# A graph network kernel: attention edge terms moved from the first count stage to TensorE in the gated pass, and gated sums taken in two column halves

## The reference

```python
# layer 0, gated: h = x, e = edge_attr_64
msg_in = concatenate([h[src], h[dst], e], axis=-1)
messages = (silu(msg_in @ w1 + b1) @ w2 + b2) * sigmoid(msg_in @ wg + bg)
agg = segment_sum(messages, dst) / maximum(deg, 1)
h_new = silu(concatenate([h, agg]) @ wu + bu)
# layer 1, mean: sums the features of the sources of each target
# layer 2, attention, twice (l = 1, 2): ea = edge_attr_128 plus loop rows
a_e = ea @ We_l @ ae_l                    # the attention edge term: one number per edge
alpha = leaky_relu(a_s[src] + a_d[dst] + a_e)
```

## Time and profile before

| What | Value |
|---|---|
| median of 3 runs | 2327.94 us (2326.16 to 2332.72) |
| span of the profiled execution, first to last instruction | 2030.3 us |
| median less span | 297.6 us |
| PE busy | 1709.1 us, 84% of the span |
| DVE busy | 1468.0 us, 72% |
| POOL busy | 985.4 us, 49% |
| ACT busy | 869.6 us, 43% |
| mean granted TensorE clock | 0.915 of full speed |
| gated pass, first gather to last addition of a window | 49.2 to 618.2 us of the span |
| first count stage, first DVE work to last addition | 659.4 to 962.8 us of the span |

### The profile page before, as it was taken

The page is one execution under the profiler, slowest core; times in us unless marked ns, Lnnn a source line. Parts: engine busy times, 40 slices in busy tenths (PEclk is TensorE's granted clock), DMA queues, the critical chain, the costliest instruction groups (busy, mean ns, idle before and its releaser), DMA issues. The chain is left out here.

```text
span 2030.3 us, 42546 instructions
## 1 busy us (share of the span) xinstructions
PE 1709.1 (84%) x13175; PEld 1366.7 (67%) x13175; DVE 1468.0 (72%) x4926; ACT 869.6 (43%) x2150; POOL 985.4 (49%) x998
## 2 busy tenths in 40 slices
PE   5699998989883799999557999956599999299996
PEld 5588877878773666677555887746478878166664
DVE  5788888888885899896667666655776664744656
ACT  2466655655554566564304444421154443411100
POOL 3777777777773000000366777735677775300000
PEclk9899999999996699999658999986699999699998
DMA  6877677777760245553352111108221111344542
GB/s 189 236 210 231 200 223 215 206 228 204 206 199 6 98 165 197 171 198 151 119 135 62 46 42 42 48 18 203 61 67 43 41 43 36 123 163 182 197 164 87
DMA packets 145068, 276.84 MB, mean 136 GB/s; under 512 B 28296, under 2 KB 88334, under 8 KB 141557
## 3 DMA queue, kind: packets, MB, share of 16 engines
q1 hardware_dynamic: 105102, 191.71, 29.2%
q0 software_dynamic: 35456, 79.88, 14.9%
q10 hardware_dynamic: 4278, 2.42, 0.5%
HBM read 228.82 MB, written 45.08 MB: 135 GB/s over the span
## 5 line engine op out<-in xcount | busy, mean ns | idle before, releaser
L1023 POOL DMA_INDIRECT gated_rows<-p_tab,src_idx x416 | 432.2, 1039 | 141.6 <-issue 130.6
L1387 POOL DMA_INDIRECT ring<-table,src_idx x384 | 383.9, 1000 | 146.0 <-issue 93.3
L2219 PE MATMUL bank<-counts,mean_xs 128*128 128x416 bf16 (+2 forms) x1350 | 219.6, 322 | 32.0 <-DVE mean_xs L1707 32.0
L1052 PE MATMUL bank<-gated_wide_q,gated_comb 128*128 128x256 f32 x832 | 219.7, 388 | 2.7 <-DMA gated_wide_q<-q_tab 2.7
L1121 ACT ACTIVATE gated_sig<-gated_pre 128x512 f32<-128x512 f32 x208 | 131.2, 631 | 211.4 <-DVE gated_pre L1193 208.7
L2219 PEld LDWEIGHTS bank<-counts,mean_xs 128*128 128x128 bf16 x1350 | 126.0, 97 | 116.4 <-issue 34.4
L1518 ACT COPY attention_counts<-bank 128x475 f32 (+1 forms) x224 | 127.2, 568 | 176.9 <-PE bank L1542 153.2
L1553 PEld LDWEIGHTS bank<-attention_counts,h_sb 128*128 128x128 f32 x900 | 157.7, 191 | 61.9 <-ACT attention_counts L1518 3.6
L1193 DVE TENSOR_TENSOR gated_pre<-bank,gated_rows 128x512 f32<-128x512 f32 x208 | 142.8, 687 | 74.9 <-PE bank L1052 43.7
L1553 PE MATMUL bank<-attention_counts,h_sb 128*128 128x232 f32 (+1 forms) x900 | 192.0, 341 | 2.0 <-DVE attention_counts L1610 1.5
L1542 PE MATMUL bank<-attention_wide_b,scratch 128*128 128x400 f32 x448 | 189.2, 504 | 0.0
(11 more groups left out here) (416 smaller groups left out, 3896.0 us busy)
## 6 DMA issues: line engine op xcount, KB each, us to landing
counts<-count_tabs SPq DMA_DIRECT2D x16, 2675.0 KB, 9.4
scratch<-in_edge_attr_dram SPq DMA_DIRECT2D x51, 512.0 KB, 4.1
count_tabs<-mean_counts SPq DMA_DIRECT2D x8, 2675.0 KB, 11.2
gated_relr<-rel_rows SPq DMA_DIRECT2D x104, 128.0 KB
gated_ids<-id_rows SPq DMA_DIRECT2D x26, 512.0 KB
gated_wide_q<-q_tab SPq DMA_DIRECT2D x208, 64.0 KB
attend_hot_lo<-low_hots SPq DMA_DIRECT2D x52, 256.0 KB, 3.4
gated_ea<-in_edge_attr_dram SPq DMA_DIRECT2D x51, 256.0 KB
```

The lines of the kernel that those rows point to most:

```text
L1023: pool.indirect_dma_start(out=rows[:, q % TICKS, c, :], out_offset=None, in_=p_tab, in_offset=bass.IndirectOffsetOnAxis(ap=src_idx[:, b, j ...
L1052: mm = pe.matmul(PRE[q % 2][:, c * 2 * P:(c + 1) * 2 * P], comb[:, u, k, c, :], wide_q[:, u, c, :], start=True, stop=True)
L1387: pool.indirect_dma_start(out=rows[:, n % RING, j, :], out_offset=None, in_=table, in_offset=bass.IndirectOffsetOnAxis(ap=src_idx[:, gathe ...
L2219: mm = pe.matmul(BANKS_D[q % ND][:, 0:width], xs[l][:, m // 3, m % 3, :], counts[:, s % 2, m // 3, at:at + width], start=(m == 0), stop=(m ...
```

## The change

1. In the gated pass SP also loads edge_attr_128 (512 KB per two batches, into free space of `h_sb`). `turn_ea` transposes two 128x128 blocks of it per tick beside the one of edge_attr_64, ACT copies them out with one 128x256 copy (`eaT`), and `turn_silu` ends with two f32 matmuls that have them as stationary and `ae_v` as moving operand (two columns). ACT copies the four numbers per partition to `ae`.
2. `ae_v` is made at the start of the gated pass instead of in the update; `ae_w` is gone.
3. `sum_up` swaps its operands: 64 columns of `hot` are stationary and the message with a column of ones (129 columns) is moving. The block j even writes partitions 0 to 63 of the bank, j odd partitions 64 to 127. The bf16 counting matmuls and the cast of `hot` are gone.
4. Since the result is now nodes by features in two halves, a batch needs one step more: ACT copies the bank out (`keep_sums`, 128x129), and PE multiplies that with a 128x64 matrix that adds the halves and transposes (`fold_halves`: a 64-column f32 matmul for the features, and one with a single stationary column for the counts). DVE adds the window one tick later.
5. The first count stage loses everything that made edge terms: the loads, `turn_ea`, `make_ae`, `copy_eaT`, `take_ae`, `sum_own`. SP's wait for the stored tables moves from the attention stage to the update before it.

```diff
@@ gated_pass
+            ea128 = flat(h_sb[:, :, :])[:, J * P:J * P + UN * J * P].rearrange("p (b j d) -> p b j d", b=UN, j=J)
+            eaT = sb("eaT", [P, TRN, 2, P])
...
-                        pe.transpose(EAT[:, 0:P], ea64[:, u, 2 * k:2 * k + 2, :].rearrange("p j d -> p (j d)"),
-                                     ident[:, :]).then_inc(ea_turned, 1)
+                        pe.transpose(EAT[:, 0:P], ea64[:, u, 2 * k:2 * k + 2, :].rearrange("p j d -> p (j d)"), ident[:, :])
+                        for c in range(2):
+                            mm = pe.transpose(EAT[:, (1 + c) * P:(2 + c) * P], ea128[:, u, 2 * k + c, :], ident[:, :])
+                        mm.then_inc(ea_turned, 1)
...
-                            mm = pe.transpose(ST[:, c * P:(c + 1) * P], silu[:, q % 2, c, :], ident[:, :])
+                            pe.transpose(ST[:, c * P:(c + 1) * P], silu[:, q % 2, c, :], ident[:, :])
+                        for c in range(2):
+                            mm = pe.matmul(ST[:, 2 * (P + c):2 * (P + c) + 2], eaT[:, q % TRN, c, :], ae_v[:, :], start=True, stop=True)
...
-                        for c in range(2):
-                            j = 2 * k + c
-                            pe.matmul(SEG[b % 2][:, 0:W], msg[:, q % 2, c, :], hot[:, u, j, :],
-                                      start=(j == 0), stop=(j == J - 1), skip_group_check=True)
-                        for c in range(2):
-                            j = 2 * k + c
-                            mm = pe.matmul(SEG[b % 2][:, W:2 * W], ones_b[:, :], hot_b[:, u, j, :],
-                                           start=False, stop=(j == J - 1), skip_group_check=True)
+                        for c, half in ((0, low), (1, high)):
+                            mm = pe.matmul(SEG[b % 2][half, 0:P + 1], hot[:, u, 2 * k + c, :], msg[:, q % 2, c, :],
+                                           start=(k == 0), stop=(k == PAIRS - 1), skip_group_check=True)
                         mm.then_inc(summed, 1)
+                    def fold_halves(b):
+                        pe.wait_ge(seg_ready, b + 1)
+                        pe.matmul(SEG[b % 2][:, FEATS], seg_s[:, b % 2, 0:P], fold[:, :], start=True, stop=True)
+                        pe.matmul(SEG[b % 2][0:1, DEGREES], seg_s[:, b % 2, P:P + 1], fold[:, :], start=True, stop=True).then_inc(folded, 1)
...
+                            if i > 7 and (i - 7) % PAIRS == PAIRS - 1:
+                                fold_halves((i - 7) // PAIRS)
                             if 0 <= i - 6 < NQ:
                                 sum_up(i - 6)
...
+                        reach(act, s_turned, q - TRN + 1)
+                        act.copy(flat(eaT[:, q % TRN, :, :]), EAT[:, P:3 * P]).then_inc(eaT_ready, 1)
...
+                        act.copy(ae[:, :, b, 2 * k:2 * k + 2], ST[:, 2 * P:2 * P + 4].rearrange("p (c l) -> p l c", l=2))
...
-                        act.copy(hot_b[:, b % UN, :, :], hot[:, b % UN, :, :]).then_inc(hot_b_ready, 1)
+                    def keep_sums(b):
+                        act.wait_ge(summed, (b + 1) * PAIRS)
+                        reach(act, folded, b - 1)
+                        act.copy(seg_s[:, b % 2, :], SEG[b % 2][:, 0:P + 1]).then_inc(seg_ready, 1)
@@ mean_build
-                        for at in pe_due(n):
-                            copy_eaT(at)
...
-                            for at in pe_due(n):
-                                turn_ea(at)
-                                if at > 0:
-                                    make_ae(at - 1)
                             count(n)
...
-                        if n is not None:
-                            for at in own_due(n):
-                                sum_own(at)
```

More of the change, by code:

```diff
@@ L161, in build_program @@
     place_a, origin_a = sb("place_a", [1, NSB * ATP], I32), sb("origin_a", [1, LAST], I32)
-    OWN = [i for i in range(10) if i % 2]
-    BY_PE = [i for i in range(SB_BATCHES) if i not in OWN]
-    assert BY_PE == [0, 2, 4, 6, 8, 10, 11, 12]
     ae_v, ae = sb("ae_v", [P, 2]), sb("ae", [P, 2, NB, J])
-    ae_w = sb("ae_w", [P, 2, P])
     w_tab, w_c = sb("w_tab", [P, NB, J]), sb("w_c", [P, NB, J])
@@ L690, in _ @@
                     clear_spent(sp)
-                    if gate:
-                        for k in range(2):
-                            sp.dma_start(we_g[:, k, :], a[f"L2_gnn_We{k + 1}"]).then_inc(ae_in, 16)
-                            sp.dma_start(ae_c[:, k:k + 1], a[f"L2_gnn_ae{k + 1}"].rearrange("(p a) -> p a", a=1)).then_inc(ae_in, 16)
+                    if not gate:
+                        for k in range(TABS):
+                            sp.wait_ge(table_stored[k], 16 * len(range(k, NSB, TABS)))
                 @block.gpsimd
@@ L714, in _ @@
                         mm.then_inc(a_made, 1)
-                        if gate and g == 1:
-                            pe.wait_ge(ae_in, 16 * 4)
-                            for k in range(2):
-                                mm = pe.transpose(bank[6][:, k * P:(k + 1) * P], we_g[:, k, :], ident[:, :])
-                            mm.then_inc(ae_turned, 1)
-                        if gate and g == 2:
-                            pe.wait_ge(ae_taken, 2)
-                            for k in range(2):
-                                pe.matmul(bank[6][:, k * P:(k + 1) * P], ae_b[:, k, :], we_T[:, k, :], start=True, stop=True)
-                                mm = pe.matmul(bank[6][:, (2 + k) * P:(2 + k) * P + 1], we_T[:, k, :], ae_c[:, k:k + 1], start=True, stop=True)
-                            mm.then_inc(ae_made, 1)
                 @block.scalar
@@ L905, in gated_pass @@
             loaded, ready = sem("loaded"), sem("ready")
-            ea64_in = [sem(f"ea64_in{u}") for u in range(UN // LB)]
+            ea64_in, ea128_in = [[sem(f"{n}_in{u}") for u in range(UN // LB)] for n in ("ea64", "ea128")]
             relr_in = [sem(f"relr_in{u}") for u in range(UN // LB)]
@@ L1031, in _ @@
                     pe.wait_ge(loaded, 16 * 6)
-                    pe.wait_ge(ready, 3)
+                    pe.wait_ge(ready, 5)
                     pe.wait_ge(split, 5 + 6)
                     pe.wait_ge(we_placed, 2)
+                    pe.wait_ge(ae_in, 16 * 4)
+                    for l in range(2):
+                        mm = pe.transpose(bank[7][:, l * P:(l + 1) * P], we_g[:, l, :], ident[:, :])
+                    mm.then_inc(ae_turned, 1)
+                    pe.wait_ge(ae_taken, 1)
+                    for l in range(2):
+                        mm = pe.matmul(bank[7][:, (2 + l) * P:(2 + l) * P + 1], we_T[:, l, :], ae_c[:, l:l + 1], start=True, stop=True)
+                    mm.then_inc(ae_made, 1)
+                    pe.wait_ge(ae_taken, 2)
                     def turn_ea(q):
@@ L1922, in apply @@
                                 mm.then_inc(applied, 1)
-                    def turn_ea(n):
-                        b = pe_batch(n)
-                        pe.wait_ge(ea_in[b // LB % (ER // LB)], 16 * (b // ER + 1 + (2 if b // LB * LB + LB == NB else 0)))
-                        reach(pe, eaT_ready, n)
-                        for j in range(J):
-                            mm = pe.transpose(EAT[:, j * P:(j + 1) * P], ea128[:, b % ER, j, :], ident[:, :])
-                        mm.then_inc(ea_turned, 1)
-                    def make_ae(n):
-                        pe.wait_ge(eaT_ready, n + 1)
-                        if n == AE_COUNT:
-                            pe.wait_ge(ae_taken, 1)
-                        b = pe_batch(n) % HALF
-                        for j in range(J):
-                            at = b * J + j
-                            mm = pe.matmul(AE[:, at:at + HALF * J + 1:HALF * J], eaT[:, n % 2, j * P:(j + 1) * P], ae_v[:, :], start=True, stop=True)
-                        mm.then_inc(ae_made, 1)
                     for k, w, size, n in block_steps(M_BLOCKS):
@@ L2394, in _ @@
                         load_lows(g)
-                    if l == 1:
-                        for k in range(TABS):
-                            sp.wait_ge(table_stored[k], 16 * len(range(k, NSB, TABS)))
                     for g in range(2, N3, 3):
```

175 lines of the change are left out of this document (51 added, 124 removed).

## The result

The changed kernel takes 2314.52 us (median of 6 runs, 2310.6 to 2321.94), the kernel before in the same comparison 2333.93 us (6 runs). The ratio is 0.9912, 95% interval 0.9889 to 0.9935: some 20 us faster. The forecast was 2346 us.

The account below looks back on a forecast made before the run. POOL's gathers were taken to bound the gated pass, full PE and DVE the count stage. With PE becoming the pass's bound, +102 us there and -84 us in the count stage gave +18 us, 2327.9 to about 2346 us; range 2294 to 2408 us.

Parts of the forecast that it names:

- B in full: Gated pass: the two half-sum matmuls overlap fully, 0.22 us instead of 0.45 per tick; 2299 us, chance 0.14.
- B in part: Gated pass: only one pass of each half-sum matmul overlaps, 0.34 us instead of 0.45; 2323 us, chance 0.22.
- Taken as unchanged: Whole kernel: 297.6 us around the profiled span stay as before, added to the new span of 2048 us.
- POOL's 2.69 us per tick: Gated pass before: POOL's gathers set the tick; PE's own pace is 2.23 us, leaving it some 0.46 us slack.
- PE's tick of 3.05 us: Gated pass after: PE's work sums to 3.05 us per tick, above POOL's 2.69, so PE becomes the bound.
- the halves: Gated pass: two f32 summing matmuls of 129 moving columns cost PE 0.45 us per tick, bounds 0.22 and 0.79.
- a change of the tiling mode drains TensorE: Gated pass: switching to narrow stationaries priced at zero; the rival with a drain adds 67 us, 2413 us, chance 0.14.
- Neither can hide behind the other, and ACT is near: First count stage: DVE at 0.84 and PE at 0.85 us a step; removing edge terms gives -84 us, bounds 68 and 95.
- Rival D: Count stage: DVE and ACT as near the bound as PE, giving back 68 us or less; 2362 us, chance 0.11.
- E: Gated pass: added work nearly hides behind POOL's gathers, tick 2.72 us; kernel at 2278 us, chance 0.04.
- the gathers that wait for DVE's L1193 line: Gated pass, sign of the forecast in the profile after: POOL's gathers wait for DVE and are no longer continuous.
- idle time ended by ACT: Gated pass, sign against the forecast: PE having such idle time would make the whole account wrong.

Follow-up runs that it names:

- e6: Kernel before, with the gated pass's gathers replaced by plain transfers of consecutive rows; 2144.07 us, ratio 0.9133.
- e7: Changed kernel, with the gated pass's gathers replaced by plain transfers of consecutive rows; 2236.29 us, ratio 0.9519 to the kernel before.
- e4: Changed kernel, with ACT's register reads in the count stage 8 at a time, not 26; 2296.74 us, ratio 0.9777 to the kernel before.
- e8: Kernel before, with ACT's register reads in the count stage 8 at a time, not 26; 2348.44 us, ratio 0.9982.
- e10: Kernel before, with DVE's share of the count stage's edge terms left out; 2345.02 us, ratio 0.9971.
- e11: Kernel before, with PE's share of the count stage's edge terms and ACT's copies of them left out; 2329.62 us, ratio 0.991.
- b0: Kernel before, unchanged, timed and profiled again; 2346.64 us, ratio 0.9995, span 2338.4 us.
- e12: Kernel before, with gathers of the gated pass at most 4 ticks ahead, not 8; 2335.87 us, ratio 1.0004.

## Why the prediction was wrong

Its sign was wrong. The sum was +102 in the pass and -84 in the count stage; measured were +29 and -45. The first two steps below made the +102, the fourth the -84. That 2315 us still lies in the stated range of 2294 to 2408 us is luck: it stands between the numbers of B in full and B in part, and neither is why.

- **"Taken as unchanged": the 297.6 us around the span.** This was the step that failed. In every other execution on record 1.8 to 2.9 us lie outside the span. A median 15% above the span of the profiled execution was a sign that the profile did not show the kernel that was timed; I booked it as a constant.
- **"POOL's 2.69 us per tick" as the tick of before, and so a slack of 0.46 us.** This step follows from the first, and it is the one that sized the term. In typical executions the tick is 3.42 us while PE's work is 2.23: the slack is 1.2 us per tick. The new work of 0.79 us (3.02 - 2.23) fits in, and 0.13 us of it shows (3.55 - 3.42), 29 us with start and draining instead of 102. e6 and e7 show this: without the pauses the tick goes from 2.44 to 3.09.
- **PE's tick of 3.05 us** was right (3.02 by its parts, 3.09 in e7 with the self term), term by term within 0.10 us. Of the terms, the folding was too low by 0.08, and the halves came to 0.47 for 0.45: 0.37 for themselves and 0.10 for entering the narrow stationary. In a folding tick the 0.10 is most likely within the folding's 0.57. The prediction's row for entering a one-column stationary showed 0.67 us from start to start and nothing to hold it against; in e7 the two passes ahead of the folding's one-column matmul take 0.26 us, where two transposes take 0.22 (L1051), so that switch may not be free either. The rule of the Trainium skill (TensorEngine Tiling (Array Packing), Key Properties) that a change of the tiling mode drains TensorE, which I had priced at nothing, agrees in direction with that 0.10 us, 21 us in 208 ticks if they lay bare; its other rule, that different tiles can load and multiply in parallel, agrees with the pairs of passes that start 6 to 7 ns apart in e7, though a fifth of the time was saved and not half.
- **"Neither can hide behind the other, and ACT is near": -84 us in the count stage.** The size was near for PE and DVE (78.6 us, e4 against e8; e10, e11: balanced). What I missed is the third engine: I took ACT's busy share for its load, and its reads of registers, which no busy share counts, were 30 us in the stage and became 51. Asking "what is late next" of PE and DVE was not enough; that step gave 45.
- Rival D named the right place and a third engine, and its sign came (252.7 us for 208 steps are 1.21 us each, over its 0.95), but with 68 us it was still too high. E, the added work hidden, came true by a mechanism that it did not have: not behind POOL but in the pauses.
- Of the signs named beforehand, the gathers that wait for DVE's L1193 line (now L1202) came; PE at 0.97 did not (0.90), and it had idle time ended by ACT (L1081 in the timeline above), which the text had said would overturn the account. It did.

## What to carry over

Before an expected slack is spent, compare the span of the profiled execution with the time that is being judged; if they are 15% apart, the profile shows another regime, and every "bound" in it has to be read again from a second profile. When two balanced engines are relieved together, look at the third one's sequencer as well: register reads, here 26 values at once, count as busy nowhere and are hidden only as long as someone else is late; 8 at a time were worth 40 us of the stage after the change and 6 before it. And a loss of 92 us in one regime can be a gain of 20 in another, so the condition belongs beside the number.

## What the runs showed of the hardware

- With 416 gathers in the gated pass, PE's semaphore updates are recorded late and in bursts: 273 of 580 by over 1 us, at most 6.7 us (b0), and ACT and DVE stand together 43 times in 500 us; with 208 or with none, at the same bytes and packets, that is gone and the kernel is 200 us faster (2147 and 2144 us against 2352 and 2349). It is not the number outstanding (e12). Their rate is the nearest that is left, but the one quick execution had all 416 at 1.34 us each and no late update, so the cause stays open. The attention stages, which gather too, are 150 us longer in b0 than in the quick execution; the count stage, which has no gathers, isn't. The traces have the same sign there: in the attention stages 74 of PE's 314 recorded updates come over 1 us late in b0 and 78 of 312 in e6, none of 409 in the quick execution, and none in the count stage of any of the three. No run took the gathers out of the attention stages.
- A read of 26 values into ACT's registers takes 1.9 or 5.6 us by turns in the kernel before, 2.7 or 10.2 us in the changed one; a read of 8 mostly 0.55 us. Reads of 14 on ACT take 1.2 or 3.1 us by turns. Why every second one is long, and why it grew, is open.
- Entering a 64-column stationary cost 0.10 us. Two f32 matmuls of 129 columns into the two column halves ran in pairs of passes with starts 6 to 7 ns apart (e7), and took 0.37 us where one behind the other would be 0.45: a pair is dearer than a single pass.
